# Attention of a two-layer decoder block on one Trainium2 core: turns, maxima and projections in 64-row halves of TensorE

## The reference

```python
x = x + _L0_attn_ref(_layernorm(x, axis=-1), ...)                       # window
x = x + _L0_xattn_ref(ctx_1024, ctx_1024, _layernorm(x, axis=-1), ...)  # cross_pad
x = x + _L0_ffn_ref(_layernorm(x, axis=-1), ...)                        # experts
x = x + _L1_attn_ref(_layernorm(x, axis=-1), ...)                       # causal
x = x + _L1_xattn_ref(_layernorm(x, axis=-1), ctx_1024, ...)            # cross_mask
x = x + _L1_ffn_ref(_layernorm(x, axis=-1), ...)                        # gated

# each attention, 16 heads of 16 columns
q, k, v = xn @ Wq + bq, y @ Wk + bk, y @ Wv + bv
scores = jnp.einsum('bhqd,bhkd->bhqk', q, k) * scale
attn = softmax(where(mask, scores, -inf), axis=-1)
out = jnp.einsum('bhqk,bhkd->bhqd', attn, v) @ Wo + bo
```

## Time and profile before

| | |
|---|---|
| median of 3 runs | 2140.37 us (2137.2 to 2140.66) |
| span of the profiled execution | 2144.3 us, 3.9 us above the median of the runs |
| PE busy | 2001.3 us, 93% |
| DVE busy | 1247.5 us, 58% |
| ACT busy | 963.5 us, 45% |
| POOL busy | 689.7 us, 32% |

### The profile page before, as it was taken

The page is one execution under the profiler, slowest core; times in us unless marked ns, Lnnn a source line. Parts: engine busy times, 40 slices in busy tenths (PEclk is TensorE's granted clock), DMA queues, the critical chain, the costliest instruction groups (busy, mean ns, idle before and its releaser), DMA issues. The chain is left out here.

```text
span 2144.3 us, 51295 instructions
## 1 busy us (share of the span) xinstructions
PE 2001.3 (93%) x17274; PEld 1546.4 (72%) x17274; DVE 1247.5 (58%) x5456; ACT 963.5 (45%) x1873; POOL 689.7 (32%) x1244
## 2 busy tenths in 40 slices
PE   8999998999976999999999889999999998999889
PEld 6777776666656999999999667777766665444377
DVE  6778886666642011110115588888878876459964
ACT  3555545656622333333333355555555553357400
POOL 3666665345552000000000545554422220013400
PEclk9999999999978999999999999999999999999999
DMA  7333332333318999999997534343233331000023
GB/s 221 115 104 108 108 112 90 98 104 119 109 52 322 399 343 340 340 346 338 341 342 291 160 127 129 127 132 114 93 96 103 109 104 47 0 0 1 0 61 97
DMA packets 209540, 334.50 MB, mean 156 GB/s; under 512 B 59501, under 2 KB 193426, under 8 KB 200306
## 3 DMA queue, kind: packets, MB, share of 16 engines
q1 hardware_dynamic: 194914, 301.82, 40.8%
q0 software_dynamic: 9552, 26.10, 4.0%
q10 hardware_dynamic: 4928, 4.72, 0.6%
HBM read 193.74 MB, written 28.05 MB: 103 GB/s over the span
## 5 line engine op out<-in xcount | busy, mean ns | idle before, releaser
L2044 ACT ACTIVATE moe_h<-moe_h_ps,moe_weights 128x128 f32<-128x128 f32 x424 | 132.4, 363 | 256.0 <-PE moe_h_ps L2012 226.2
L1339 ACT ACTIVATE causal_prob<-causal_ps 128x768 f32<-128x768 f32 (+1 forms) x192 | 168.8, 879 | 112.9 <-PE causal_ps L1592 112.0
L2477 PE MATMUL ffn_prod_ps<-x_sb,ffn_weights 128*128 128x512 f32 x480 | 209.5, 596 | 7.0 <-ACT ffn_sig_q L2463 7.0
L2076 DVE TENSOR_TENSOR moe_y<-moe_y_ps,moe_weights 128x256 f32<-128x256 f32 x53 | 22.5, 424 | 328.2 <-PE moe_y_ps L2024 328.2
L2012 PE MATMUL moe_h_ps<-moe_h,moe_weights 128*128 128x128 f32 x1696 | 198.0, 275 | 0.0
L1955 POOL DMA_DIRECT2D moe_y_dram<-moe_y x71 | 39.4, 554 | 492.1 <-DVE moe_y L2076 492.1
L2012 PEld LDWEIGHTS moe_h_ps<-moe_h,moe_weights 128*128 128x128 f32 x1696 | 193.6, 192 | 0.1
L2477 PEld LDWEIGHTS ffn_prod_ps<-x_sb,ffn_weights 128*128 128x128 f32 x480 | 90.6, 191 | 123.6 <-issue 109.3
L1029 DVE CUSTOM_DVE_ANT_0 causal_masked<-causal_ps,causal_causal_mask 128x256 bf16<-128x256 f32 (+1 forms) x512 | 152.3, 354 | 42.5 <-PE causal_ps L1558 38.5
L1029 DVE CUSTOM_DVE_ANT_0 window_masked<-window_ps,window_window_mask 128x160 bf16<-128x160 f32 x512 | 135.5, 320 | 58.6 <-PE window_ps L1558 56.0
L1339 ACT ACTIVATE window_prob<-window_ps 128x640 f32<-128x640 f32 x128 | 89.9, 703 | 97.4 <-PE window_ps L1592 96.5
(11 more groups left out here) (404 smaller groups left out, 4699.0 us busy)
## 6 DMA issues: line engine op xcount, KB each, us to landing
moe_weights<-moe_w_in SPq DMA_DIRECT2D x53, 2180.0 KB, 9.1
q_pair<-parts SPq DMA_DIRECT2D x512, 128.0 KB
parts<-moe_w_in SPq DMA_DIRECT2D x17, 2180.0 KB
k_pair<-parts SPq DMA_DIRECT2D x256, 128.0 KB
k_pair<-parts SPq DMA_DIRECT2D x256, 38.5 KB
moe_y_dram<-moe_y POOLq DMA_DIRECT2D x71, 128.0 KB, 3.4
moe_rows<-moe_slots_dram SPq DMA_DIRECT2D x53, 128.0 KB, 3.0
x_before_ffn_dram<-x_sb SPq DMA_DIRECT2D x16, 256.0 KB, 2.1
```

Of the source, the lines that this page charges most:

```text
L1339: nc.scalar.activation(out, src, ACT.Exp).then_inc(expd, 1)
L2044: nc.scalar.activation(out[:, f, :], psum[:, f // 2, (f % 2) * TM:(f % 2) * TM + TM], ACT.Gelu, bias=bias[:, f:f + 1]).then_inc(done, 1)
L2477: op = nc.tensor.matmul(prod_ps[:, slot, f, :].rearrange("p (b t) -> p b t", b=2), w[:, k, at:at + P], x_cols(n // GROUPS, k), start=(k == ...
```

## The change

It does the following; experts and feed-forward are untouched.

- Turns of the normalised rows, of the maxima and of the last rows run in 64-row halves: twice the instructions, each with 64 columns moving instead of 128.
- The products for query, key, value and output run in halves too. `halves` has two phases: in the first each half of the array takes the products of its own bank, in the second the halves are crossed. The second phase waits for the first (`proj_half`, `out_half`), and stands a slot later, behind other work.
- The value products `pv` come in two blocks of two (`first_quads`, `last_quads`), so `prob` has four places instead of two.
- The banks are three pairs with other uses: `psa` (turned rows, key, maxima, value products) and `psb` (query, value, heads, output).
- The output product is made in slots 0 and 1 of the next step instead of slot 7.
- DVE divides by the sums behind `row_max` of slot 6 instead of ahead of it, adds the output in slot 1, takes `low_part` of the query in slot 3 and that of the key in slot 4 (before: 2 and 3).
- ACT's order of the step is written out anew.

```diff
-        prob = sb("prob", [P, 2, 2, 2, S + P], F32)
+        prob = sb("prob", [P, NQ, 2, 2, S + P], F32)
-        pso = pb("pso", [P, 2, 512])
-        misc = pb("misc", [P, 2, 512])
+        psa = pb("psa", [P, 2, 512])
+        psb = pb("psb", [P, 2, 512])
...
                     for i in range(PAIRS_H):
+                        if active(ref, 1):
+                            row_max(t, ref, i)
                         if i == 6 and active(ref, 3):
...
-                        if active(ref, 1):
-                            row_max(t, ref, i)
-                        if i == 0 and active(ref, 4) and not added_first:
+                        if i == 1 and active(ref, 4):
                             add_output(t, ref, 4)
...
-                        if i == 2 and active(ref, 0):
-                            low_part(q_parts[par], q_ps, layer_at(ref).bq, q_hi, q_lo, t, S)
...
+                        if i == 3 and active(ref, 1):
+                            split_max(t, ref, 1, 0)
                         if i == 3 and active(ref, 0):
+                            low_part(q_parts[par], q_ps, layer_at(ref).bq, q_hi, q_lo, t, S)
+                        if i == 4 and active(ref, 0):
                             L = layer_at(ref)
                             low_part(k_parts[par], k_ps(par, L), L.bk, k_hi, k_lo, t, L.nk)
...
+                def turn_halves(out, rows):
+
                     for k in range(KC):
                         for s in range(ST):
-                            op = nc.tensor.transpose(xT_ps[:, k, s * P:s * P + P], xn[par][:, s, k * P:k * P + P], ident[:])
-                    op.then_inc(xT_mm, 1)
+                            for ab in range(2):
+                                op = nc.tensor.transpose(out[:, ab, k * ST + s], rows[rows_of[ab], s, k * P:k * P + P],
+                                                         ident[rows_of[ab], rows_of[ab]])
+                    return op
...
+                def early_maxima(t, ref):
+
+                    wait(pe, k_lo, upto(t, ref, 0))
+                    wait(pe, m_ev, upto(t, ref, 2, 2))
+                    if in_tail(ref, 5):
+                        pe.wait_ge(last_ev, tail_item(t, 5) + 1)
+                    max_out(t, 1, 0)
...
+                def halves(phase, out, lhs, rhs):
+
+                    for k in range(KC):
+                        for ab in range(2):
+                            f = (ab + phase) % 2
+                            op = nc.tensor.matmul(out(f), lhs(f, k)[rows_of[ab]], rhs(f, k)[rows_of[ab]],
+                                                  start=(phase == 0 and k == 0), stop=(phase == 1 and k == KC - 1),
+                                                  skip_group_check=True)
+                    return op
...
+                        if i == 0 and active(ref, 4) and not narrow:
+                            output(t, ref, 0)
+                        if i == 1 and active(ref, 4):
+                            output(t, ref, 1)
+                        if i == 2 and now and not narrow:
+                            query(t, ref, 0)
+                        if i == 3 and active(ref, 2):
+                            late_maxima(t, ref)
+                        if i == 3 and now:
+                            query(t, ref, 1)
...
+                        if i == 5 and active(ref, 1) and not narrow:
+                            early_maxima(t, ref)
+                        if i == 5 and now:
+                            value(t, ref, 1)
```

610 lines of the change are left out of this document (347 added, 263 removed).

## The result

The changed kernel takes 2264.8 us (median of 4 runs, 2259.2 to 2273.9) against 2139.1 before (median of 4; with the first three of them it was the 2140.4 that the prediction counts from): ratio 1.0589, 95% interval 1.0563 to 1.0614. The direction was as forecast, the size was not: +126 us measured, +36 forecast, and the time lies above the range (2118 to 2222).

The account below looks back on a forecast made before the run. The prediction took three loops to bound the kernel: PE's work, DVE's row maxima and the query's copies over the DMAs. Terms -10 + 0 + 22 + 10 + 14 = +36 us on 2140.4 gave 2176 us, range 2118 to 2222.

Parts of the forecast that it names:

- Full products in halves, 0.9 a phase: PE's query, key, value and output products: halves overlap, taking 1.75 to 1.8 instead of 1.93, 0.9 a phase.
- The rival of halves that don't overlap: Every float32 product costs 3.5 at worst, up to 2490 us; chance 0.10, including crossed phases that wait for one another.
- that of the weight loads: Rival: full products expose weight loads and halves hide them, up to 0.5 less a product, about 2145 us; chance 0.04.
- The relief from value products in two blocks (0.3) and from the small turns: PE's work per narrow step: 0.3 from two visits fewer to 32-column mode, 0.24 from half turns.
- Narrow steps, -0.7 a window step, 0 a causal one: Self-attention steps: -10 us over 15 window steps, 0 over 15 causal steps, where DVE is fuller.
- DVE's work from the last maxima to the first sets a floor: Window steps: DVE's 3.36 between slot 7's and slot 0's maxima stays, so only 0.3 of 1.1 removed there counts.
- Cross_mask, +1.55 a step: The loop over query, low part and copies lengthens to 17.0 against 15.46: +22 us over 14 steps.
- late maxima 0.25: Cross_mask: PE's late maxima between the query's two phases, counted as 0.25 of the 4.05 there.
- Cross_pad without routing, +2.4 a step: Four cross_pad steps: the query and copies loop takes 16.4 to 17.8 against 14.70, +10 us.
- Cross_pad with routing: Ten cross_pad steps: +1.4 each, +14 us, since 1.2 of routing products already lay within the loop before.
- Start and drain, +-3: Eight steps in which pipelines fill or empty: ±3 us.
- Costed at nothing: POOL's cuts, the four places of prob and ACT's new order lie beside the chains: no cost.

Follow-up runs that it names:

- e4_whole: The changed kernel with its full products undivided, each whole where its second phase stood, the first phase left out: 2366.7 us, ratio 1.106 to the kernel before.
- e8_back_to_back: The changed kernel with both phases of every full product one behind the other where the second phase stood: 2394.8 us, ratio 1.120 to the kernel before.
- e2_late_first: The changed kernel with the late maxima of wide steps ahead of the query's first phase, so ahead of the last value products: 2252.9 us, 1.0517.
- e10_fill_sized: The changed kernel plus useless identity matmuls on PE in wide steps, cut to the number that fits into its waits: 2243.9 us, 1.0475.
- e11_route_later: The changed kernel with the routing products of cross_pad steps moved behind the query's second phase: 2255.4 us, 1.0531.
- e7_order: The changed kernel with late maxima earlier, early maxima's key wait dropped in cross layers, query's second phase earlier in wide steps, VectorE's order fitted: 2191.9 us, 1.0264.
- e9_pad_first: e7_order with GpSimd's copy of the padding row moved to the start of its step: 2182.3 us, 1.0201.
- e12_order_fill: e9_pad_first with a few useless filling matmuls on PE where it still waits in wide steps: 2171.7 us, 1.0139.

## Why the prediction was right in direction and wrong in size

The range was missed because two sums left out a wait or products that stood in the chain, and because there was no term for the clock.

- **Full products in halves, 0.9 a phase:** right. Pairs overlap, a phase takes 0.7 to 0.95, and no crossed phase waits for its partner: none stands in the list of waits. The rival of halves that don't overlap is out. So is that of the weight loads: a whole product takes 1.92 in e4_whole (184.66 to 186.58), two phases take 1.8 to 1.9, and nothing near 0.5 was hidden in it. The relief from value products in two blocks (0.3) and from the small turns was not measured apart.
- **Narrow steps, -0.7 a window step, 0 a causal one:** right, -0.97 and +0.15. That DVE's work from the last maxima to the first sets a floor was a fair reading; e4_whole and e8_back_to_back add that most of the gain is cover for the maxima, which the prediction did not count as such (it priced halves at switching, 0.15 each). The term came out near for a partly wrong reason, so that was in part luck. In causal steps the first nine grew by 0.37: PE waits there for the normalised rows (7.0 in 8 waits, 0.8 in 4 before), which VectorE now brings later than PE wants them.
- **Cross_mask, +1.55 a step:** measured +4.2. The chain as named is right: each wait forecast stands in the list, with its releaser. From the query's end to slot 6 it is 4.5 as forecast, to the copies' landing 2.0 and 6.45 as forecast. The step that failed is "late maxima 0.25" in the sum to the query's end, 8.5: they had to wait 1.0 more for the value products' eviction (ScalarE's L1407, which empties the shared pair). That gives 9.5 (9.7 as read) and a step of 18.1. Moving them ahead (e2_late_first) gave one step of 17.4 at full clock, but no shorter mean. The second failing is a missing term, and the prediction gave no reason for leaving it out: the clock. PE is idle for a fifth of these steps, and they lose granted clock, another 1.2 a step (e10_fill_sized), up to 4.75 in single steps (22.84 against 18.09).
- **Cross_pad without routing, +2.4 a step:** +3.0, at a clock of 0.90 to 0.96; the chain was near, and how much of the 0.6 is clock was not separated.
- **Cross_pad with routing, "+1.4, a little less than in cross_mask":** measured +4.4, the costliest miss (44 us for 14). The loop over query and copies had been worked out for steps without routing, 16.4 to 17.8. This step of the prediction failed: the routing products stand between the query's phases, so their 1.8 (0.5 of it the wait behind them) had to be added to that loop, 18.2 to 19.6. The rest up to 21 fits the clock (0.83 to 0.92 in these steps): in e11_route_later, without the products in the loop, steps at full clock take 17.6 to 18.2, near the 16.4 to 17.8 of the sum. The prediction took them to be in the longer step of before already; but there they were issued behind the query, and not in this loop. e11_route_later took 1.7 off these steps.
- **Start and drain, +-3:** mis-sized. The steps between layers, the start and the drains cost some 29 together; no experiment took them apart.
- **Costed at nothing:** GpSimd's and ScalarE's work. Fair for the changed kernel; once the query came early, the padding row on GpSimd was next in line (e7_order, e9_pad_first).

The warning of the Trainium skill that was cited in the prediction ("TensorEngine Tiling (Array Packing)", section "PSUM Bottleneck") agrees with the causal steps: PE relieved, step +0.15, VectorE at 88%. Another line of that page of the Trainium skill bears on the missed wait: its section "Gotcha 1: PSUM Pressure" says that row tiling increases the pressure on PSUM, since row tiles write to different banks. There are four pairs of banks before and after (the list of changes says three), with `ps1` and `ps2` as they were. Before, turned rows, key and maxima took one bank of `misc`, query, value and output the other, and the value products had a pair of their own; in halves each of them takes both banks of a pair, so the maxima share one with the value products. The late maxima behind the value products show the price, 1.0 a step.

What stays open: e12_order_fill is still 32 us above the kernel before. In its profile, 36 above that of before, 5 stand ahead of the first head turns, 5 between the two runs, 19 in cross_pad and 15 in cross_mask steps, -13 in window steps, some 4 elsewhere; how much of the cross steps' part is clock and how much GpSimd's sending of rows was not separated. Half turns and value products in two blocks were not tried apart, and neither were halves in the order of the kernel before: so nothing shows what the halves alone are worth there.

## What to carry to other kernels

- When a product is split and its second half moved later, what counts is when the last half ends, and here everything between the halves, small products of other work included, is on that loop. Add the items up for each kind of step; don't scale from a similar kind.
- When the same buffers are dealt out anew among their users, list every neighbouring pair of users in program order: where the second has to wait for the first one's eviction, add that wait to the chain (1.0 here).
- On a kernel whose TensorE is nearly always busy, price idle time on it twice, once as the wait and once by the clock, and read step lengths only beside the granted clock. A removed wait can be lost again in the mean (e2_late_first: 17.4 at full clock, 19.66 on average). Pieces small enough to go into every slot can be worth more than their arithmetic.

## What the chip did that was not expected

- The granted clock as a follower of PE's idle time. With all other engines' work alike, steps took 18.1 at 0.99 and 22.8 at 0.74 (means over stretches at the two levels, 2.4 and 1.2 GHz), though the longest wait listed for these steps is 1.3. "TensorE: Matmul & The Clock Gate", Part 1, of the Trainium skill says that this gate follows how busy the engine has recently been; here e10_fill_sized agrees: useless matmuls in the waits brought cross_mask's clock from 0.90 to 0.99 and took 21 us off the whole.
- Filling must be measured in place: one float32 product of 128 by 128 by 128 took 0.26, where turns of the same shape had taken 0.15. The records show why: six products are twelve records in 1.54, four turns are four records in 0.59. Six instead of three cost nearly all of the gain (2261 against 2244).
